# One copy for two heads' turned probabilities, and three steps moved in the order of the work

## The chip, the cores and the metric

The kernel runs on one core of one Trainium2 chip. The metric is the device time of one execution in microseconds (us); lower is better. A core has five engines that run side by side and wait for each other by semaphores: TensorE (PE in the rows, with its weight loads as PEld), VectorE (DVE), ScalarE (ACT), GpSimd (POOL) and SyncE (SP), which here only starts transfers. All of them share an on-chip memory of 128 partitions, the arena, and PE, DVE and ACT also reach PE's output memory, eight banks of 128 x 512 f32.

## The reference, cut to what matters

Two layers over 8 sequences of 512 tokens with 256 features. The first (a gated recurrence and a routed feed-forward net) is not touched. The second layer is, per sequence, a recurrence with a 16 x 16 state per head, times the SiLU of a block of attention and experts. Both read the normed input:

```python
x = x + s * g                        # s, g: the first layer's two branches
xn = _layernorm(x, axis=-1)
s = _L1_attn_ref(xn, ...)            # recurrence: state*w + k v, read out by r
g = _silu(_L1_ffn_ref(xn, ...))      # causal attention, then 8 experts + 1 shared
x = x + s * g
# inside _L1_ffn_ref, 16 heads, t = 512:
att = jnp.einsum('bhqd,bhkd->bhqk', q, k) / jnp.sqrt(jnp.float32(D))
att = jnp.where(mask, att, jnp.float32(-jnp.inf))
att = jax.nn.softmax(att, axis=-1)
y = jnp.einsum('bhqk,bhkd->bhqd', att, v)
```

## The kernel before, in words

Phases a and b compute the first layer and leave its branch `s` in rows in DRAM and its branch `g` sorted by expert in DRAM (`gate_rows`). Phase c computes the second layer, one sequence after another (`b` from 0 to 7). On each engine the order of the instructions is written out by hand and is strict; a wait holds up everything behind it on that engine. For each sequence phase c goes through three stages.

`before_attention` computes the projections. PE writes the last ones in the order of the list `QKV`: sp0, sp1, q2 to q7, lat. DVE turns each pair of heads' queries by their positions in `rotate` and so frees the bank. In between stand the first two attention steps: PE does `scores(b, 0)` after q5 and `scores(b, 1)` after q6, and DVE does the maxima of their rows, `highest(b, 0)` and `highest(b, 1)`, after its rotations of q5 and q6.

`attention` has 32 steps, `i` from 0 to 31. A step is one pair of heads (`i // 4`) and one tile of 128 queries (`qt = i % 4`), so that it has 1, 2, 3 or 4 tiles of 128 keys. Each step goes through these instructions:

- PE `scores(i)` (L1241, and the mask, L1244) into banks 0 and 1 or 2 and 3; it needs the exponentials of step i-2, which read the same banks.
- DVE `highest(i)` (L1822), one maximum for both heads.
- ACT `exp` (L1623), one instruction for each head, out of the bank into the arena, with the row sums.
- PE `turn_probs(i)` (L1258), `qt + 1` transposes for each head, head 0 into bank 5 and head 1 into bank 6.
- ACT `keep` (L1632), one copy for each head, out of the bank into the tile `turned`.
- PE `weigh_values` (L1295), in every second group of four steps, which multiplies the turned probabilities of four heads by the values.

PE's order in iteration i is `scores(i)`, `turn_probs(i - 2)`, `weigh_values(i - 3)` where there is one; ACT's is both copies of step i-2, then both exponentials of step i. Around this PE also reduces the recurrence's products (L1268), and DVE runs the 32 units of the recurrence, each a scan (L1842) and an outer product (L1835).

`experts` runs nine experts, `e` from 0 to 8. PE does `up(e)` and `down(e)` (L1382) and DVE `hidden(e)` (L1987, the product that `down(e)` needs), the sums of the experts' rows (L2073), and then `between(e)`: one or two units of the recurrence, and the head of the next sequence in pieces. `head_gate` (L1730) multiplies the rows of `s` by those of `g`, `head_sum` (L1734) adds the residual, `head_stats` (L1739) takes means and variances, `head_shift` (L1751) and `head_lerp` (L1764) come later. The rows of `g` are fetched by GpSimd with four indirect transfers (L2104), issued after its recurrence product of unit 24.

Of the kernel before, what the change touches and what calls it, by code (L numbers as in the profile page):

```python
# [11 lines left out]
ACT = mybir.ActivationFunctionType  # L12
X = mybir.AxisListType.X

P = 128
# [949 lines left out]
def phase_c(nc, io, dram, mem, const, psum, bank, pos_all, second, second_loads, weights_in, out):  # L965
# [3 lines left out]
    with ExitStack() as ctx:  # L969
# [42 lines left out]
        turned_at = mem.at  # L1012
        turned = [mem.take(NT, T) for _ in range(HGROUP)]
        neg_max, row_sum, row_inv = mem.take(STEPS), mem.take(STEPS), mem.take(STEPS)
# [140 lines left out]
        def _(pe):  # L1155
# [91 lines left out]
            def turn_probs(b, i):  # L1247

                qt = i % NT
                if i == 0:  # L1250
                    pe.wait_ge(v_read, pre.read(b, "q7"))
                for half in range(2):
                    s = 2 * i + half
                    pe.wait_ge(s_exp, STEPS * b + (s + 1))
                    if s >= 2:
                        pe.wait_ge(s_keep, STEPS * b + (s - 1))
                    for kt in range(qt + 1):
                        last = nc.tensor.transpose(bank[5 + half][:, kt * P:(kt + 1) * P], probs[s % PROBS][:, kt * P:(kt + 1) * P], ident)  # L1258
                    last.then_inc(s_turn, 1)
# [61 lines left out]
            def before_attention(b, ended):  # L1321
# [38 lines left out]
                for name in QKV:  # L1360
                    i = int(name[-1]) if name != "lat" else 0
                    if name[0] == "q":
                        query(b, i)
                        if name in ("q5", "q6"):
                            scores(b, int(name[1]) - 5)
                    elif name == "lat":
# [160 lines left out]
        def _(act):  # L1527
# [88 lines left out]
            def attention(b):  # L1616
# [8 lines left out]

                def keep(s):
                    i, half = s // 2, s % 2
                    h, qt = 2 * (i // NT) + half, i % NT
                    act.wait_ge(s_turn, STEPS * b + (s + 1))
                    if h >= HGROUP and h % HGROUP == 0:  # L1630
                        act.wait_ge(pv_mm, CHUNKS * b + (NT * (h // HGROUP - 1) + qt + 1) + CHUNKS)
                    nc.scalar.activation(turned[h % HGROUP][:, 0:qt + 1, qt * P:(qt + 1) * P],  # L1632
                                         bank[5 + half][:, 0:(qt + 1) * P].rearrange("p (k c) -> p k c", c=P),
                                         ACT.Copy).then_inc(s_keep, 1)

# [14 lines left out]
                for i in range(PSTEPS + LAG):  # L1650
# [6 lines left out]
                    if LAG <= i < PSTEPS + LAG:  # L1657
                        keep(2 * (i - LAG))
                        keep(2 * (i - LAG) + 1)
                    if i < PSTEPS:  # L1660
# [55 lines left out]
        def _(v):  # L1716
# [145 lines left out]
            def before_attention(b, ended):  # L1862
# [58 lines left out]
                for name in QKV:  # L1921
# [5 lines left out]
                    if name[0] == "q":  # L1927
                        rotate(m + 1)
                        if name in ("q5", "q6"):
                            highest(b, m - 5)  # L1930
                v.wait_ge(w_step, 2 * b + 2)
# [51 lines left out]
            def experts(b, final):  # L1983
# [46 lines left out]
                def between(e):  # L2030
                    if not final:
                        if e == 1:
                            head_gate(b + 1)
                        elif e == 2:
                            head_sum(b + 1)
                        elif e == 3:
                            head_stats(b + 1)
                    for n in EXPERT_UNITS.get(e, ()):
                        unit(b, n)
                    if not final:  # L2040
                        if e == 4:
                            head_shift(b + 1)
                        elif e == 6:
                            head_lerp(b + 1)
                    elif e == 6:
                        ln_inv(b, 0)
                    elif e == 7:
                        ln_scale(b, 0)
                        ln_gate(b, 0)
# [247 lines left out]
```

## Time and profile before

| | us |
|---|---|
| median of 3 runs | 2175.03 |
| lowest and highest run | 2170.23, 2177.49 |
| the profiled execution's own time | 2173.18 |
| its span, first to last instruction | 2171.3 |

The mean granted TensorE clock over the span is 0.971 of full speed. The span holds some 2 us less than the profiled execution's own time, and that execution lies 1.85 us below the median. Times in the rows are microseconds from the span's start.

### The profile page before, as it was taken

The numbers are of one execution on the slowest core, as the hardware profiler recorded it, in microseconds if no ns is written. First come the engines' busy times: TensorE is split into PE (matmuls) and PEld (weight loads), VectorE is DVE, ScalarE is ACT, GpSimd is POOL, SyncE is SP. The second block draws the span as 40 slices with busy tenths as digits, with TensorE's granted clock in tenths as the row PEclk, the third lists the DMA queues.
The fourth block names the chain that finished last, engine by engine and source line by source line (L and its number), as shares of the span: only waits on it lengthen the run. The fifth ranks groups of instructions, "written<-read, shape, count | busy, mean of one in ns | idle before, by whom it ended". The sixth has DMA issues, their size and how long they took to land.

```text
span 2171.3 us, 37412 instructions
## 1 busy us (share of the span) xinstructions
PE 2023.1 (93%) x11786; PEld 1237.3 (57%) x11787; DVE 1736.1 (80%) x2890; ACT 978.4 (45%) x2532; POOL 840.8 (39%) x666
## 2 busy tenths in 40 slices
PE   7998599999889999999999999999999999999996
PEld 4554399998446545644564465456445544654563
DVE  5998466665398888889978988888898788888886
ACT  3544244443247236623833472275238235723841
POOL 1335300000353345346334633553463346336531
PEclk9999799999799999999999999999999999999998
DMA  6544521211412212212321122123022211211220
GB/s 180 154 136 147 166 59 51 58 51 51 134 46 65 58 49 60 62 37 54 81 72 39 50 64 54 49 66 81 16 68 65 69 39 54 59 54 49 73 56 10
DMA packets 145728, 151.20 MB, mean 70 GB/s; under 512 B 47664, under 2 KB 105648, under 8 KB 145584
## 3 DMA queue, kind: packets, MB, share of 16 engines
q1 hardware_dynamic: 138288, 136.73, 22.8%
q0 software_dynamic: 3072, 8.41, 1.2%
q10 hardware_dynamic: 4224, 4.19, 0.7%
q8 instruction: 84, 1.38, 0.3%
q14 instruction: 60, 0.49, 0.1%
HBM read 121.71 MB, written 27.43 MB: 69 GB/s over the span
## 4 chain that ended last, share of the span: by engine, by line
PE 35%; issue 16%; POOL 10%; DVE 9%; ACT 3%; DMA 1%; POOLq 0%; DVEq 0%; ACTq 0%
PE bank L1382 8%; PE bank L1241 6%; PE bank L1258 5%; PE bank L1295 3%; PE bank L1395 3%; POOL arena L2131 3%; PE bank L1268 2%; POOL arena L2143 2%; POOL arena L2146 2%; DVE arena L1842 2%; PE bank L1244 2%; PE bank L1174 2%; ACT arena L1623 2%; POOL arena L2123 2%; DMA arena<-gate_rows,arena 1%
## 5 line engine op out<-in xcount | busy, mean ns | idle before, releaser
L2123 POOL TENSOR_TENSOR arena<-arena 128x512 f32<-128x512 f32 x256 | 341.1, 1337 | 559.1 <-DVE arena L1842 545.2
L1382 PE MATMUL bank<-arena 128*128 128x256 f32 (+1 forms) x1120 | 384.4, 498 | 20.5 <-DVE arena L1987 20.5
L1842 DVE TENSOR_TENSOR_SCAN arena<-arena 128x512 f32<-128x512 f32 x256 | 356.1, 1391 | 1.1
L1174 PE MATMUL bank<-arena 128*128 128x512 f32 (+2 forms) x768 | 350.8, 603 | 1.0 <-ACT arena L1562 1.0
L1623 ACT ACTIVATE arena<-bank,arena 128x128 f32<-128x128 f32 (+3 forms) x512 | 266.3, 530 | 171.1 <-DVE arena L1822 171.1
L1382 PEld LDWEIGHTS bank<-arena 128*128 128x128 f32 x1120 | 214.4, 195 | 179.0 <-issue 131.0
L1822 DVE TENSOR_REDUCE arena<-bank 128x2 f32<-128x256 f32 (+3 forms) x256 | 208.4, 814 | 51.7 <-PE bank L1244 51.0
L1241 PE MATMUL bank<-arena 64*128 64x128 f32 (+3 forms) x1024 | 208.2, 483 | 41.0 <-ACT arena L1623 28.2
L1174 PEld LDWEIGHTS bank<-arena 128*128 128x128 f32 (+2 forms) x768 | 138.0, 187 | 185.0 <-issue 164.4
L1835 DVE TENSOR_TENSOR arena<-arena 128x512 f32<-128x512 f32 x256 | 220.7, 864 | 11.7 <-DMA arena<-values 10.1
L1632 ACT ACTIVATE arena<-bank 128x128 f32<-128x128 f32 (+3 forms) x512 | 196.5, 439 | 40.2 <-PE bank L1258 39.3
L1258 PE MATMUL bank<-arena 128*128 128x128 f32 x1280 | 184.5, 275 | 2.3 <-DVE arena L1902 2.3
L283 PE MATMUL bank<-arena 128*128 128x512 f32 x384 | 174.3, 608 | 0.4 <-ACT arena L354 0.4
L1580 ACT ACTIVATE arena<-bank 128x512 f32<-128x512 f32 x72 | 42.7, 593 | 262.1 <-PE bank L1382 255.1
L1576 ACT ACTIVATE arena<-bank 128x512 f32<-128x512 f32 (+1 forms) x96 | 57.2, 596 | 213.9 <-PE bank L1174 213.7
L691 PE MATMUL bank<-arena 128*128 128x128 f32 x1248 | 147.8, 277 | 5.1 <-DVE arena L791 4.1
L691 PEld LDWEIGHTS bank<-arena 128*128 128x128 f32 x1248 | 147.3, 194 | 7.6 <-issue 4.4
L2146 POOL TENSOR_TENSOR arena<-arena 128x512 f32<-128x512 f32 x72 | 100.1, 1391 | 122.0 <-DVE arena L1905 118.8
L1241 PEld LDWEIGHTS bank<-arena 64*128 64x128 f32 x1024 | 77.8, 184 | 121.8 <-issue 49.6
L1258 PEld LDWEIGHTS bank<-arena 128*128 128x128 f32 x1280 | 137.7, 142 | 9.7 <-issue 6.1
L700 PE MATMUL bank<-arena 128*128 x624 | 141.1, 379 | 0.1
L354 ACT ACTIVATE arena<-bank 128x512 f32<-128x512 f32 x160 | 81.8, 611 | 109.2 <-PE bank L283 103.5
(207 smaller groups left out, 3032.4 us busy)
## 6 DMA issues: line engine op xcount, KB each, us to landing
arena<-values SPq DMA_DIRECT2D x256, 256.0 KB, 3.4
arena<-in_L_attn_h SPq DMA_DIRECT2D x16, 512.0 KB, 11.3
arena<-in_W1T SPq DMA_DIRECT2D x8, 1024.0 KB
arena<-in_W2T SPq DMA_DIRECT2D x8, 1024.0 KB
sorted_rows<-arena SPq DMA_DIRECT2D x42, 128.5 KB, 10.4
arena<-sorted_rows SPq DMA_DIRECT2D x40, 128.5 KB, 2.1
arena<-in_b2row SPq DMA_DIRECT2D x40, 128.0 KB, 2.9
gate_rows<-arena SPq DMA_DIRECT2D x39, 128.0 KB, 1.7
```

The costliest lines, as they stand in the source:

```text
L283: last = nc.tensor.matmul(bank[3 * (n % 2) + q][:, :], gru_w[layer][:, k, q * D + m * P:q * D + (m + 1) * P], source(b, u)[:, k, :], start ...
L691: last = nc.tensor.matmul(zT_bank[u % 2][half][:, (f % 4) * P:(f % 4 + 1) * P], w1_now[u % 2][:, c, f * P:(f + 1) * P], nT[u % 2][:, c, :] ...
L1174: last = nc.tensor.matmul(dst[rows, :], w, x, start=(n == 0), stop=(n == len(pairs) - 1))
L1241: nc.tensor.matmul(bank[2 * (i % LAG) + half][:, 0:n], qT[rows, p, qt * P:(qt + 1) * P], ckvT[rows, 0:n], start=True, stop=False)
L1258: last = nc.tensor.transpose(bank[5 + half][:, kt * P:(kt + 1) * P], probs[s % PROBS][:, kt * P:(kt + 1) * P], ident)
L1382: last = nc.tensor.matmul(dst[o], w, x, start=first, stop=last_one)
L1623: nc.scalar.activation(probs[s % PROBS][:, 0:n], bank[2 * (i % LAG) + half][:, 0:n], ACT.Exp, bias=neg_max[:, s:s + 1], accum_out=row_sum[ ...
L1632: nc.scalar.activation(turned[h % HGROUP][:, 0:qt + 1, qt * P:(qt + 1) * P], bank[5 + half][:, 0:(qt + 1) * P].rearrange("p (k c) -> p k c ...
L1822: nc.vector.tensor_reduce(neg_max[:, 2 * i:2 * i + 2], psum[:, at:at + 1024].rearrange("p (h k) -> p h k", h=2)[:, :, 0:n], X, ALU.max, ne ...
L1835: nc.vector.tensor_tensor(kv[n % 2], copies[n % COPIES], proj["k"][:, n // HD, :], ALU.mult).then_inc(kv_done, 1)
L1842: nc.vector.tensor_tensor_scan(state[n % STATES][:, 1:T + 1], proj["w"][:, m, :], kv[n % 2], VEC["init"][:, m * HD + j:m * HD + j + 1], AL ...
L2123: nc.gpsimd.tensor_tensor(prods[(n + 2) % PRODS], state[n % STATES][:, 0:T], proj["r"][:, m, :], ALU.mult).then_inc(prod_done, 1)
```

## The change

Four edits, without any arithmetic being added or left out:

- The two copies of a step become one: `keep(i)` reads banks 5 and 6 in one instruction and writes both heads' tiles. It waits for both heads' transposes, and raises its semaphore by 2. The four `turned` tiles become views of one tile at the same place.
- In `turn_probs` the wait for the copies of the step before stands once, ahead of the first head, and asks for both heads; before, each head waited for its own.
- `scores(b, 1)` moves from behind q6 to behind q7 on PE, and `highest(b, 1)` from behind the rotation of q6 to behind that of q7 on DVE.
- In `between`, `head_gate` moves from e = 1, ahead of unit 26, to e = 2, behind unit 27; `head_sum` moves from e = 2, ahead of unit 27, to e = 3, right ahead of `head_stats`, which stays.

```diff
-        turned = [mem.take(NT, T) for _ in range(HGROUP)]
+        turned_all = mem.take(HGROUP, NT, T)
+        turned = [turned_all[:, i, :, :] for i in range(HGROUP)]
...
                     pe.wait_ge(s_exp, STEPS * b + (s + 1))
-                    if s >= 2:
-                        pe.wait_ge(s_keep, STEPS * b + (s - 1))
+                    if i and half == 0:
+                        pe.wait_ge(s_keep, STEPS * b + 2 * i)
...
-                        if name in ("q5", "q6"):
-                            scores(b, int(name[1]) - 5)
+                        if name in ("q5", "q7"):
+                            scores(b, (int(name[1]) - 5) // 2)
...
-                def keep(s):
-                    i, half = s // 2, s % 2
-                    h, qt = 2 * (i // NT) + half, i % NT
-                    act.wait_ge(s_turn, STEPS * b + (s + 1))
+                def keep(i):
+                    h, qt = 2 * (i // NT), i % NT
+                    act.wait_ge(s_turn, STEPS * b + (2 * i + 2))
                     if h >= HGROUP and h % HGROUP == 0:
                         act.wait_ge(pv_mm, CHUNKS * b + (NT * (h // HGROUP - 1) + qt + 1) + CHUNKS)
-                    nc.scalar.activation(turned[h % HGROUP][:, 0:qt + 1, qt * P:(qt + 1) * P],
-                                         bank[5 + half][:, 0:(qt + 1) * P].rearrange("p (k c) -> p k c", c=P),
-                                         ACT.Copy).then_inc(s_keep, 1)
+                    at = h % HGROUP
+                    nc.scalar.activation(turned_all[:, at:at + 2, 0:qt + 1, qt * P:(qt + 1) * P],
+                                         psum[:, 5 * 512:7 * 512].rearrange("p (h k c) -> p h k c", h=2, c=P)[:, :, 0:qt + 1, :],
+                                         ACT.Copy).then_inc(s_keep, 2)
...
-                        keep(2 * (i - LAG))
-                        keep(2 * (i - LAG) + 1)
+                        keep(i - LAG)
...
-                        if name in ("q5", "q6"):
-                            highest(b, m - 5)
+                        if name in ("q5", "q7"):
+                            highest(b, (m - 5) // 2)
...
-                    if not final:
-                        if e == 1:
-                            head_gate(b + 1)
-                        elif e == 2:
-                            head_sum(b + 1)
-                        elif e == 3:
-                            head_stats(b + 1)
+                    if not final and e == 3:
+                        head_sum(b + 1)
+                        head_stats(b + 1)
                     for n in EXPERT_UNITS.get(e, ()):
                         unit(b, n)
+                    if not final and e == 2:
+                        head_gate(b + 1)
```

## Rows read from the trace of the kernel before

**Rows 1.** The page's busy times: engine, us (share of span), instructions.

```profile
PE 2023.1 (93%) x11786; PEld 1237.3 (57%) x11787; DVE 1736.1 (80%) x2890; ACT 978.4 (45%) x2532; POOL 840.8 (39%) x666
```

**Rows 2.** Who waited for whom, whole span: us in total, times, longest.

```profile
DVE arena L1730 <- DMA arena<-gate_rows,arena: 41.3, 8, 7.8
ACT arena L1632 <- PE bank L1258: 39.3, 60, 1.1
...
DVE arena L1788 <- PE bank L1306: 36.7, 8, 5.1
...
PE bank L1241 <- ACT arena L1623: 28.2, 57, 1.9
...
PE bank L1382 <- DVE arena L1987: 20.5, 8, 2.9
```

**Rows 3.** Timeline of DVE, experts of sequence 6: start, us, what [idle before, releaser].

```profile
1912.60 1.65 DVE L2073 SCALAR_TENSOR_TENSOR arena<-bank,arena 128x256 f32<-128x256 f32 x4
1919.07 1.23 DVE L1730 TENSOR_TENSOR arena<-arena 128x1024 f32<-128x1024 f32 x1 [4.83 <-DMA arena<-gate_rows,arena]
...
1929.24 1.40 DVE L1739 BATCH_NORM_STATS2 arena<-arena 128x6 f32<-128x256 f32 x4
...
1949.32 0.68 DVE L1987 TENSOR_TENSOR arena<-arena,bank 128x512 f32<-128x512 f32 x1
```

**Rows 4.** Timeline of PE in the same experts.

```profile
1909.22 10.60 PE L1382 MATMUL bank<-arena 128*128 128x256 f32 x32
1922.73 7.12 PE L1382 MATMUL bank<-arena 128*128 128x256 f32 x16 [2.90 <-DVE arena L1987]
...
1948.36 3.73 PE L1382 MATMUL bank<-arena 128*128 128x256 f32 x16
```

**Rows 5.** Stretches after the stall: us, PE, PEld, DVE, ACT, POOL busy, clock, DMA.

```profile
1131.95:1135.35 3.40, 3.34 (x8) 2.71 (x9) 3.40 (x7) 0.00 (x0) 0.35 (x1) 0.50 0.40 80
...
1330.21:1333.61 3.40, 3.35 (x12) 2.37 (x13) 3.40 (x6) 0.00 (x0) 0.35 (x1) 1.00 0.27 77
...
1922.67:1926.07 3.40, 3.34 (x9) 2.70 (x10) 3.40 (x7) 0.00 (x0) 0.36 (x1) 0.58 0.38 77
1926.07:1930.07 4.00, 4.00 (x13) 1.44 (x15) 4.00 (x10) 0.60 (x1) 1.46 (x1) 0.93 0.02 0
```

**Rows 6.** Timeline of PE, experts of sequence 3, after its stall.

```profile
1347.92 1.09 PE L1301 MATMUL bank<-arena 128*128 128x128 f32 x8 [0.63 <-ACT arena L1535]
1357.60 2.00 PE L1382 MATMUL bank<-arena 128*128 128x256 f32 x8 [0.48 <-DVE arena L1987]
```

**Rows 7.** The copies by shape, whole span: busy, mean ns, idle before.

```profile
L1632 ACT ACTIVATE arena<-bank 128x512 f32<-128x512 f32 x128 | 69.9, 597 | 21.4 <-PE bank L1258 21.4
...
L1632 ACT ACTIVATE arena<-bank 128x128 f32<-128x128 f32 x128 | 28.9, 285 | 17.8 <-PE bank L1258 17.8
```

**Rows 8.** Timeline of PE and ACT, attention steps 13 to 15 of sequence 6.

```profile
1837.75 1.04 PE L1258 MATMUL bank<-arena 128*128 128x128 f32 x8
...
1838.39 1.09 ACT L1632 ACTIVATE arena<-bank 128x512 f32<-128x512 f32 x2 [0.77 <-PE bank L1258]
...
1839.37 0.48 ACT L1623 ACTIVATE arena<-bank,arena 128x256 f32<-128x256 f32 x1
...
1840.44 1.13 PE L1241 MATMUL bank<-arena 64*128 64x512 f32 x4 [0.36 <-ACT arena L1623]
```

**Rows 9.** Timeline of PE and ACT, the last attention steps of sequence 6.

```profile
1877.45 0.84 PE L1258 MATMUL bank<-arena 128*128 128x128 f32 x6
...
1881.70 1.09 ACT L1632 ACTIVATE arena<-bank 128x512 f32<-128x512 f32 x2 [0.91 <-PE bank L1258]
```

**Rows 10.** Timeline of PE and DVE, the first attention steps of sequence 6.

```profile
1806.86 0.70 PE L1241 MATMUL bank<-arena 64*128 64x256 f32 x4 [1.03 <-DVE arena L1902]
...
1814.26 1.19 DVE L1822 TENSOR_REDUCE arena<-bank 128x2 f32<-128x1024 f32 x1
...
1816.99 0.87 PE L1241 MATMUL bank<-arena 64*128 64x256 f32 x4 [1.46 <-ACT arena L1623]
```

## The prediction, made before the changed kernel ran

> **What bounds the kernel now.** I read the busy times first [rows 1]. The reader should see that TensorE is busy for 93% of the span, and VectorE, at 80%, is the next. A cut elsewhere is worth only what TensorE stops waiting or stops running slowly. The list of waits says where TensorE waits [rows 2]: 28.2 us in 57 places for ScalarE's exponentials, and 20.5 us in 8 places for `hidden` on VectorE. Seven of those 8 follow a wait of VectorE itself, the 41.3 us in 8 places for the rows of `gate_rows` at `head_gate` (the eighth, of 7.8 us, stands ahead of the first sequence and is not touched).
>
> Then I read the timelines around both. In the experts of sequence 6 VectorE ends a sum at 1914.25 (1912.60 + 1.65), stands idle for 4.83 us until the gathered rows are there at 1919.07, and then works without a pause up to `hidden(8)` at 1949.32 [rows 3]. TensorE ends `up(4)` at 1919.82 (1909.22 + 10.60) and waits 2.90 us for `hidden(3)`, which stands behind the stall [rows 4]. The sixteen matmul records after the wait took 7.12 us; thirty-two before it took 10.60, or 5.3 for sixteen. The windows say why: the granted clock was 0.58 in the 3.4 us after the wait and 0.93 in the next 4 [rows 5], a mixture of 1.2 and 2.4 GHz. A stretch of length L at mean clock c costs (1 - c) x L against full speed, here 0.42 x 3.4 + 0.07 x 4 = 1.71 us. The same two windows after the other six stalls give 1.71, 1.71, 3.10, 0, 1.70 and 1.71; the clock of 0.50 and that of 1.00 are the extremes [rows 5]. Together 11.6 us.
>
> The stage after the experts begins with VectorE waiting for TensorE, 36.7 us in 8 places [rows 2]. So at the end of the experts TensorE is late, not VectorE, and time that TensorE saves there moves on into the next stage.
>
> **The gate and the sum moved.** No instruction is added or removed. Behind the sum that ends at 1914.25 VectorE now goes on with unit 26, `hidden(3)`, the next sums and unit 27. How long is that? From the gate at 1919.07 to `head_stats` at 1929.24 [rows 3] are 10.2 us: gate and sum at 1.2 us each, and twice one unit, one `hidden`, one group of sums. Half of the remaining 7.8 is 3.9, of which the sums are 1.6 and `hidden` 0.6 [rows 3], so a unit is 1.7. The gate stands at 1914.25 + 3.9 + 1.7 = 1919.9, and the rows were there at 1919.07. The transfers are issued by GpSimd behind unit 24, which the edit does not move. So the stall of 4.8 us should vanish, with 0.8 us to spare. Should the rows come somewhat later, the next that is late is `hidden(4)`, at about 1921.7, which TensorE needs only after `down(3)`, `up(5)` and a reduction, at about 1926: there are 4 us of cover.
>
> Is the whole stall then gain? TensorE runs from 1919.82 without the 2.90 and at full clock without the 1.71: its last matmul ends at 1947.5, not 1952.1. `down(8)` is the second half of the last 3.73 us [rows 4], so it starts at 1945.6. It needs `hidden(8)`, whose end moves by the stall from 1950.0 to 1945.2. That fits with 0.4 us to spare, so TensorE stays the bound, barely. Sequence 3 is the check: its clock never fell [rows 5], and it had 1.1 us of waits behind VectorE instead [rows 6], and its experts took as long as the others. Sum: seven waits of 2.86 us on average are 20.0, the clock 11.6, sequence 3's later waits 1.1, together 32.7 us less. The bounds are 7 x 3.6 = 25, if waits like those of sequence 3 come back everywhere, and 7 x 4.83 = 34, the whole stall.
>
> The Trainium skill (TensorE: Matmul & The Clock Gate, "HAM oscillation") says that idle gaps in TensorE's stream bring the low clock and that the restart pays for them. The trace agrees, six times of seven [rows 5]; without the clock's part the sum would be 21 us and not 33.
>
> **One copy for two.** 512 copies become 256. By shape a copy of 512 elements takes 597 ns and one of 128 takes 285 [rows 7]: 0.81 ns an element and 181 ns fixed. One instruction for 2 x 512 should take 181 + 832 = 1013 ns, against 1.09 us for the pair [rows 8], which already overlaps. So a step saves 0.07 us of ScalarE, 18 us over 256 steps, and for most of them ScalarE has idle time anyway (45% busy [rows 1]). The Trainium skill (ScalarE: Activation LUTs, "What ACT_TABLE_LOAD costs") gives a fixed cost of 186 ns and an overlap of 93 ns between neighbours. By its figures the saving would be 93 ns a step and 24 us in all, an estimate and again only of ScalarE's own time.
>
> The price is the start. A pair could begin when head 0 was turned; the one copy waits for head 1 too. At 1837.75 TensorE turns step 11 with eight transposes, the first copy starts at 1838.39 after a wait for the first four, and the exponential of step 13 starts at 1839.37 [rows 8]. The eighth transpose ends at 1838.79, so the one copy runs from 1838.83 to 1839.84, where the pair ended at 1839.48: the exponentials come 0.36 us later. `scores(15)` already waits 0.36 us for them [rows 8], so this is on the path. The pattern needs a step of four key tiles with no `weigh_values` behind it: steps 11, 19 and 27 (step 3 too, but there its successor has over 0.5 us of slack). Worked through the timelines, step 11's delay is partly taken back at the next wait for exponentials, leaving 0.2; step 19's stays, 0.36. At step 27 and the end, no scores come between the turns of steps 29 and 30, so TensorE waits for the copy itself at 1877.45 [rows 9], 0.65 in all. The last copy, at 1881.70 after 0.91 us of idle time [rows 9], ends 0.3 later and the last `weigh_values` waits 0.2. That is 1.4 us a sequence and 11.3 us over eight. Bounds: nothing, if small slack that I can't see takes it up, and 2.0 a sequence or 16 us, if each of the four places costs its full delay and a bit more. I take 11. The single wait of `turn_probs` for both copies asks nothing more, as the one copy ends both at once; merging the tiles into one moves no address.
>
> **The scores and the maximum moved.** TensorE's wait of 1.03 us ahead of `scores(1)` [rows 10] goes, since q7 fills it. But VectorE works without a pause through this stage, and the order of its instructions is all that changes there: `highest(3)` still starts at 1814.26, and the wait of 1.46 us ahead of `scores(5)` ends with the exponentials of step 3, which follow it [rows 10]. `highest(1)` comes 1.2 us later, and behind it on ScalarE stand the copies of step 0 and the exponentials of step 2. Those have about 0.9 us of idle time ahead of the exponentials of step 3 to catch up in. I take 0 us, with bounds of -0.3 and +0.3 a sequence, or 2.4 us each way.
>
> **Sum.** -32.7 + 11.3 + 0 = -21.4. The profiled execution's 2173.2 gives 2151.8. The median is 1.85 higher: 2153.6, rounded to 2153.
>
> **The rivals.**
> A, as above: 2153, with its own range 2146 to 2160.
> B, the one copy costs nothing, since the later exponentials are absorbed: 2175 - 33 = 2142. For it: in most of the 57 waits the exponential itself had waited for VectorE, not for a copy. Against it: the 0.36 of [rows 8] follows right behind the copy.
> C, VectorE becomes the bound of the experts: with 0.4 us to spare at `hidden(8)`, and sum and statistics now in one piece ahead of unit 28, waits of 1.1 us as in [rows 6] come in all seven: 2153 + 7.7 = 2161.
> D, the other sign: the one copy delays TensorE at every step by the second head's transposes, 0.11 us for each key tile, 1.1 us for a group of four steps, 8.8 a sequence, 70 in all: 2175 - 33 + 70 = 2212. It decides from 33 / 64 = 0.5 us a group on. For it: TensorE has hardly any slack. Against it: ScalarE stood idle for its transposes ahead of only 60 of 512 copies [rows 2]; elsewhere both heads had been turned long before.
> E, ScalarE's saved time lies on the path throughout: 2175 - 33 - 18 = 2124. Against it: the 57 waits are only 28.2 us in all, and the copies have no more than a share in them. The skill's saving of 93 ns would give 2118, by the rule above.
> F, the change does not do what it says: the gather is still late, or `head_sum` and `head_stats` in one piece hold up `hidden(5)` as long as the gate held up `hidden(3)`. Then only the copy's cost remains, 2175 + 0 to 11.
>
> **Chances.** A 0.50, B 0.17, C 0.17, D 0.06, E 0.05, F 0.05. Within 0.3% (6.5 us, about what a measurement of this kernel can tell from no change) falls half of F, 0.03. Slower are D and the rest of F, 0.08. Faster are A, B, C and E, 0.89. The range for 8 in 10 takes A, B and C with the bounds of the unknown costs: 2175 - 34 - 2 = 2139 below and 2175 - 25 + 16 = 2166 above; I take 2138 to 2166.
>
> **What would show it.** Right: no idle time ahead of L1730 in seven sequences, no wait of TensorE for L1987 in the middle of the experts, a clock of 1.00 there, and experts 4.6 us shorter. In attention, 256 copies of about 0.39 to 1.01 us, the wait ahead of `scores(15)` at about 0.7 us and not 0.36, and a stage longer by 1.4 us. Wrong: a new wait ahead of L1301 or of the last `down`, copies that take more than the sum of two, or an attention stage that is not longer. The most likely error is the size of the copy's price; the next is the clock, which follows idle time in ways that six cases of seven don't settle.

## The result and the profile after

The changed kernel takes 2181.34 us (median of 11 executions, lowest 2179.45), against 2174.68 us for the kernel before (11 executions beside it, 2167.43 to 2178.96). The ratio is 1.0034, 95% interval 1.0023 to 1.0045: slower by 7.4 us (the medians alone differ by 6.7), just past the 0.3% that can be told from no change. The forecast was 2153 us with a range of 2138 to 2166. One execution of 2630.08 us, and one of 5120.62 us in a later experiment, were disturbed and are left out of the ratios.

The profiled execution has a span of 2180.5 us (2171.3 before) at a mean clock of 0.969 (0.971), and its own time is 2182.27. The page's busy times, which answer to [rows 1]:

```profile
PE 2037.5 (93%) x11786; PEld 1242.7 (57%) x11787; DVE 1754.9 (80%) x2890; ACT 963.8 (44%) x2276; POOL 833.6 (38%) x666
```

ScalarE has 256 instructions and 14.6 us less. But VectorE, with the same 2890 instructions, is busy for 18.8 us more, and TensorE, with the same 11786, for 14.4 us more. Some instructions therefore take longer than they did. The list of waits of the changed kernel (us in total, times, longest), beside [rows 2]:

```profile
DVE arena L1788 <- PE bank L1307: 36.7, 8, 5.1
...
PE bank L1242 <- ACT arena L1624: 22.9, 42, 1.2
...
PE bank L1259 <- ACT arena L1633: 11.3, 45, 0.5
...
PE bank L1302 <- ACT arena L1536: 11.2, 8, 2.4
...
PE bank L1383 <- DVE arena L1987: 3.4, 7, 0.5
```

The 20.5 us of waiting for `hidden` are down to 3.4, and the wait of VectorE for `gate_rows` is gone in all seven places. TensorE waits 5.3 us less for the exponentials. In exchange it waits in 45 places for the copy itself ahead of `turn_probs` (L1259), where it had not waited at all, and 11.2 us ahead of L1302 (3.2 us in 2 places before), which turns the next sequence's normed input and comes after `head_stats` and `head_shift`.

**Stages.** Two instructions of VectorE mark two stages of a sequence. The attention stage runs from the start of L1788 to the start of L1936 (projections and attention), the experts' stage from there to the next L1788. The first L1936 has no L1788 ahead of it, so seven attention stages have a length; the low clock is counted for all eight. In the table the attention stage is given for sequences whose clock stayed at 1.00 in it, and where there are several, as the shortest of them. Low clock is counted as in the prediction, (1 - c) x L summed over windows of 4 us in the 92 us ahead of L1936.

| | before | after |
|---|---|---|
| attention stage at clock 1.00, us | 119.48 (five, to 119.82) | 121.38 (one) |
| sequences of 8 with low clock there, and how much | 3, 1.7 us each | 6 with 3.4 us, 1 with 1.7 |
| attention stage in these, us | 120.74 | 123.0 to 123.4; 122.06 |
| experts' stage, us | 77.12 to 77.22, once 78.50 | 75.21 to 75.24 |
| last experts' stage, us | 69.60 | 70.04 |

Over the seven experts' stages with a successor the changed kernel is 14.9 us shorter. Over the seven attention stages behind them it is 19.7 us longer, the last experts are 0.4 longer, and the first L1936 starts 3.7 us later. That is +8.9 of the 9.2 us between the spans. The 3.7 are not all the change's: in the profiles of all fourteen kernels of this document the first L1936 starts between 694.8 and 701.0 us (697.3 before, 701.0 here).

**Where half of the gate's gain went.** VectorE's timeline in the experts of sequence 6, beside [rows 3] (everything in this sequence stands 7.2 us later than in the kernel before):

```profile
1924.16 1.65 DVE L2071 SCALAR_TENSOR_TENSOR arena<-bank,arena 128x256 f32<-128x256 f32 x4
1925.73 2.76 DVE L1842 TENSOR_TENSOR_SCAN arena<-arena 128x512 f32<-128x512 f32 x1
1928.41 0.66 DVE L1835 TENSOR_TENSOR arena<-arena 128x512 f32<-128x512 f32 x1
1929.00 2.11 DVE L1730 TENSOR_TENSOR arena<-arena 128x1024 f32<-128x1024 f32 x1
...
1936.38 1.28 DVE L1842 TENSOR_TENSOR_SCAN arena<-arena 128x512 f32<-128x512 f32 x1
```

GpSimd's timeline in the same stretch:

```profile
1924.11 0.94 POOL L2102 DMA_INDIRECT arena<-gate_rows,arena  x1 [0.30 <-issue]
1925.07 2.33 POOL L2121 TENSOR_TENSOR arena<-arena 128x512 f32<-128x512 f32 x2
1928.57 1.46 POOL L2121 TENSOR_TENSOR arena<-arena 128x512 f32<-128x512 f32 x1 [1.17 <-DVE arena L1842]
```

The second of the two products in the row of 1925.07, taken by itself:

```profile
1926.30 1.10 POOL L2121 TENSOR_TENSOR arena<-arena 128x512 f32<-128x512 f32 x1
```

And TensorE's, beside [rows 4, 6]:

```profile
1945.60 1.09 PE L1302 MATMUL bank<-arena 128*128 128x128 f32 x8 [1.26 <-ACT arena L1536]
...
1955.27 2.00 PE L1383 MATMUL bank<-arena 128*128 128x256 f32 x8 [0.49 <-DVE arena L1987]
```

VectorE has no idle time ahead of `head_gate`, as forecast. But the scan of unit 27 takes 2.76 us, where an undisturbed one takes 1.28 (the last row of VectorE's), and the gate takes 2.11 us, where it took 1.23 [rows 3]. Both run beside GpSimd: its products of units 25 and 26 had piled up behind the four transfers and run back to back from 1925.07 to 1927.40, and the next runs from 1928.57 to 1930.03. The scan overlaps the first pair for 1.67 us and is stretched by 1.48; the gate overlaps the next product for 1.03 us and is stretched by 0.88. This makes 2.36 us of the 4.8 that the stall took. In the kernel before, the product of unit 25 ran from 1917.15 to 1918.42, while VectorE stood idle for the gathered rows, and those of units 26 and 27 one at a time, at 1921.65 and 1926.65, and neither the gate nor the scans of units 26 and 27 were stretched. TensorE now waits 1.26 + 0.49 us in these experts.

The Trainium skill (SBUF — State Buffer, "Who interferes with whom") says that a VectorE instruction with two inputs in the arena contends with a GpSimd instruction that reads it, for a port pair that only one of them holds at a time, and that the order in which they are issued decides who is blocked. The lengths in the trace agree to within 0.2 us: blocked until 1927.40 and then 1.28 long, the scan would end at 1928.68, and ended at 1928.49; the gate would end at 1931.26, and ended at 1931.11. Read with the starts in the trace, the order does not agree. The product of unit 26 started at 1926.30, 0.57 us after the scan, and yet ran its 1.10 us while the scan was held. The next product started during L1835 and got in ahead of the gate; an experiment below has the same starts to within 0.01 us and the other outcome in six of seven sequences.

**Where the copy costs.** By shape, the copies of the changed kernel, beside [rows 7]:

```profile
L1633 ACT ACTIVATE arena<-bank 128x1024 f32<-128x1024 f32 x64 | 66.0, 1031 | 59.9 <-PE bank L1259 36.2 <-issue 23.7
...
L1633 ACT ACTIVATE arena<-bank 128x256 f32<-128x256 f32 x64 | 24.8, 387 | 5.0 <-PE bank L1259 2.8
```

The same place as in [rows 8], ScalarE of sequence 6 first and then TensorE:

```profile
1844.11 1.03 ACT L1633 ACTIVATE arena<-bank 128x1024 f32<-128x1024 f32 x1 [1.11 <-issue]
1845.04 0.46 ACT L1624 ACTIVATE arena<-bank,arena 128x256 f32<-128x256 f32 x1
```

```profile
1842.99 1.04 PE L1259 MATMUL bank<-arena 128*128 128x128 f32 x8
...
1845.29 0.41 PE L1259 MATMUL bank<-arena 128*128 128x128 f32 x2 [0.20 <-ACT arena L1633]
...
1846.10 1.13 PE L1242 MATMUL bank<-arena 64*128 64x512 f32 x4 [0.40 <-ACT arena L1624]
...
1884.62 0.85 PE L1259 MATMUL bank<-arena 128*128 128x128 f32 x6 [0.48 <-ACT arena L1633]
```

From the start of the turn of step 11 to `scores(15)` it is now 1846.10 - 1842.99 = 3.11 us, where it was 1840.44 - 1837.75 = 2.69 [rows 8]. That is 0.42 us, where 0.36 was worked out. The delay shows in two waits, 0.20 ahead of the next turn and 0.40 ahead of the scores, not in the one of 0.7 that was forecast. The last row is the turn of step 30, which follows its predecessor without `scores` between them.

**The clock.** Windows of 2 us in the first attention steps of sequence 5 (columns as in [rows 5]), and TensorE's timeline there, beside [rows 10]:

```profile
1616.00:1618.00 2.00, 1.92 (x14) 1.16 (x13) 1.97 (x2) 0.06 (x1) 1.47 (x2) 1.00 0.02 4
1618.00:1620.00 2.00, 0.60 (x2) 0.29 (x2) 2.00 (x6) 0.05 (x1) 1.83 (x2) 0.65 0.00 0
1620.00:1622.00 2.00, 1.07 (x3) 0.51 (x4) 1.97 (x2) 2.00 (x9) 1.92 (x2) 0.50 0.00 0
1622.00:1624.00 2.00, 2.00 (x10) 0.85 (x6) 0.53 (x1) 0.53 (x2) 2.00 (x2) 0.50 0.03 8
1624.00:1626.00 2.00, 2.00 (x14) 1.42 (x12) 2.00 (x4) 1.62 (x4) 2.00 (x3) 0.64 0.04 0
```

```profile
1614.93 0.70 PE L1242 MATMUL bank<-arena 64*128 64x256 f32 x4
...
1619.40 0.69 PE L1259 MATMUL bank<-arena 128*128 128x128 f32 x2 [1.48 <-DVE arena L1902]
1621.02 2.08 PE L1242 MATMUL bank<-arena 64*128 64x512 f32 x4 [0.93 <-ACT arena L1624]
...
1626.37 0.70 PE L1242 MATMUL bank<-arena 64*128 64x256 f32 x4 [0.25 <-ACT arena L1624]
```

The wait ahead of `scores(1)` is gone, as meant, and the 1.46 us ahead of `scores(5)` [rows 10] are down to 0.25. In their place TensorE waits 1.48 us ahead of the first turn and 0.93 ahead of `scores(3)`, with 0.7 us of work between them. The clock falls to 0.50, that is 1.2 GHz, at about 1618.6, during the first of them, and is back at 1.00, 2.4 GHz, some 7 us later. The four matmul records of `scores(3)` (two matmuls, with two records each) take 2.08 us, where the same four at full clock take 1.13 (the row of `scores(15)` above). In the other sequences such a pair of waits (0.86 to 1.51 us, then 0.93 to 1.19) stands there too, but the clock falls at different points: before the second wait, in it or, in sequence 6, 1.2 us behind it, and in sequence 1, with waits of 0.89 and 1.18, not at all.

### The profile page after: what moved, and what is told of

Read it like the earlier page. It is cut to its first block, busy times and chain, and to the rows that moved or that the text cites. A ratio compares the mean times of both kernels' runs of the same rounds, so it can differ in the third digit from the quotient of the medians.

```text
span 2180.5 us, 37068 instructions
## 1 busy us (share of the span) xinstructions
PE 2037.5 (93%) x11786; PEld 1242.7 (57%) x11787; DVE 1754.9 (80%) x2890; ACT 963.8 (44%) x2276; POOL 833.6 (38%) x666
## 4 chain that ended last, share of the span: by engine, by line
PE 45%; issue 11%; DVE 9%; ACT 4%; POOL 4%; DMA 0%; ACTq 0%; POOLq 0%; DVEq 0%
PE bank L1383 14%; PE bank L1242 6%; PE bank L1175 5%; PE bank L1259 5%; ACT arena L1624 3%; PE bank L1296 3%; PE bank L1396 3%; PE bank L1269 3%; PE bank L1245 2%; PE bank L1453 1%; POOL arena L2129 1%; PE bank L1281 1%; DVE arena L1866 1%; ACT arena L1633 1%; DVE arena L1822 1%
## 5 line engine op out<-in xcount | busy, mean ns | idle before, releaser
L2121 POOL TENSOR_TENSOR arena<-arena 128x512 f32<-128x512 f32 x256 | 330.6, 1297 | 571.3 <-DVE arena L1842 556.6
L1383 PE MATMUL bank<-arena 128*128 128x256 f32 (+1 forms) x1120 | 374.1, 486 | 3.4 <-DVE arena L1987 3.4
L1842 DVE TENSOR_TENSOR_SCAN arena<-arena 128x512 f32<-128x512 f32 x256 | 363.8, 1421 | 1.1
L1242 PE MATMUL bank<-arena 64*128 64x128 f32 (+3 forms) x1024 | 215.8, 499 | 26.2 <-ACT arena L1624 22.9
L1835 DVE TENSOR_TENSOR arena<-arena 128x512 f32<-128x512 f32 x256 | 222.2, 870 | 11.6 <-DMA arena<-values 10.0
L1633 ACT ACTIVATE arena<-bank 128x256 f32<-128x256 f32 (+3 forms) x256 | 181.2, 708 | 98.5 <-PE bank L1259 63.3
L1259 PE MATMUL bank<-arena 128*128 128x128 f32 x1280 | 192.8, 283 | 20.0 <-ACT arena L1633 11.3
L1259 PEld LDWEIGHTS bank<-arena 128*128 128x128 f32 x1280 | 141.7, 145 | 33.8 <-issue 23.2
L691 PE MATMUL bank<-arena 128*128 128x128 f32 x1248 | 148.5, 277 | 5.1 <-DVE arena L791 4.1
L2144 POOL TENSOR_TENSOR arena<-arena 128x512 f32<-128x512 f32 x72 | 102.5, 1423 | 121.9 <-DVE arena L1905 118.7
```

The costliest lines, as they stand in the source:

```text
L691: last = nc.tensor.matmul(zT_bank[u % 2][half][:, (f % 4) * P:(f % 4 + 1) * P], w1_now[u % 2][:, c, f * P:(f + 1) * P], nT[u % 2][:, c, :] ...
L1242: nc.tensor.matmul(bank[2 * (i % LAG) + half][:, 0:n], qT[rows, p, qt * P:(qt + 1) * P], ckvT[rows, 0:n], start=True, stop=False)
L1383: last = nc.tensor.matmul(dst[o], w, x, start=first, stop=last_one)
L1633: nc.scalar.activation(turned_all[:, at:at + 2, 0:qt + 1, qt * P:(qt + 1) * P], psum[:, 5 * 512:7 * 512].rearrange("p (h k c) -> p h k c", ...
L1835: nc.vector.tensor_tensor(kv[n % 2], copies[n % COPIES], proj["k"][:, n // HD, :], ALU.mult).then_inc(kv_done, 1)
L1842: nc.vector.tensor_tensor_scan(state[n % STATES][:, 1:T + 1], proj["w"][:, m, :], kv[n % 2], VEC["init"][:, m * HD + j:m * HD + j + 1], AL ...
```

## The experiments

Each ratio is against the kernel before, with its 95% interval, and a difference to it in us is the ratio's; the medians of the kernel before beside them were 2174.15 (the first four), 2172.41 (the next four) and 2174.35 us (the last four). Experts' stages and attention stages are those defined above, each read from one profiled execution of the kernel; where the attention stages at clock 1.00 differ, the shortest is given.

**The parts alone.** Only the hunk in `between`:

```diff
+                    if not final and e == 3:
+                        head_sum(b + 1)
+                        head_stats(b + 1)
                     for n in EXPERT_UNITS.get(e, ()):
                         unit(b, n)
+                    if not final and e == 2:
+                        head_gate(b + 1)
```

> Before, with head_gate and head_sum moved alone. Theory 1 (each edit has its own price; VectorE became the bound of the experts because the scan of unit 27 and the gate now run beside GpSimd's products): experts of 75.2 us in place of 77.2, seven times, so 14 us less than before in all, 2161; the gate takes 2.1 us and TensorE waits some 1.3 us for the norm of the next sequence. Theory 2 (the gain is only held back by the one copy): the full 4.6 us a sequence, 33 us less, 2142.

Measured: 2152.68 us, 0.9905 [0.989, 0.9919], so 20.7 us faster, between the 14 of the one theory and the 33 of the other. The gate takes 2.11 us in all seven sequences and the experts' stages are 74.8 us, 2.4 shorter than before. They sum to 17.9 us; 2.2 more come from the attention stages, of which one of eight has low clock and not three.

Only the merged copy, with `turned_all`, the one wait and `keep(i)`:

> Before, with the one copy and its single wait on TensorE alone. Theory 1: the later start costs 2.0 us a sequence in attention and 0.4 behind it, 19 us in all, 2194, and the granted clock at the start of attention stays as before. Theory 2 (the copy costs what was predicted, 1.4 us a sequence, and the rest is TensorE's clock at the start of attention): 2186.

Measured: 2191.65 us, 1.008 [1.0066, 1.0094], 17.4 us slower. The attention stage at clock 1.00 is 121.47 us (the longest of six 122.45), 2.0 longer than before, and the experts' stage 77.6, 0.44 longer. The low clock comes ahead of two of eight L1936, against three before.

Only `scores(b, 1)` and `highest(b, 1)` moved behind q7:

> Before, with scores(b, 1) and highest(b, 1) behind q7 alone. Theory 1: the two waits of TensorE that take the place of one bring the low clock at the start of attention in most sequences and for longer, and the stage gets 0.5 to 1.5 us longer: 4 to 12 us more, about 2182. Theory 2 (the low clock needs the one copy as well): no difference to before, 2175.

Measured: 2176.43 us, 1.0012 [1.0002, 1.0023], 2.6 us slower. The low clock comes as the first theory says, but at less than its price: all eight attention stages have 3.4 us of it, and the seven that can be measured last 120.7 to 121.2 us. The experts' stages are 77.1 to 77.2 us although in six of seven the clock was 1.00 throughout them. In the kernel before most of them had 1.7 us of low clock and the same length.

The gate, the sum and the scores, without the merged copy:

> The changed kernel with two copies as before: scores, maximum, gate and sum moved. Theory 1 (prices add up): 14 less and 7 more, about 2168. Theory 2: 2142 plus nothing.

Measured: 2156.04 us, 0.9919 [0.9905, 0.9932]. Put beside the first of these kernels, the moved scores bring nothing; the median is 3.4 us higher, with intervals that overlap. All eight attention stages have low clock, seven of them 1.7 us, and last 119.7 to 120.1 us, so that this much of it costs some 0.25 us a stage here.

**What in the copy costs.** The kernel before, its two copies kept, but each waiting for both heads, and one wait in `turn_probs`:

```diff
-                    if s >= 2:
-                        pe.wait_ge(s_keep, STEPS * b + (s - 1))
+                    if i and half == 0:
+                        pe.wait_ge(s_keep, STEPS * b + 2 * i)
...
-                    act.wait_ge(s_turn, STEPS * b + (s + 1))
+                    act.wait_ge(s_turn, STEPS * b + (2 * i + 2))
```

> Before, still with two copies a step, but each waits for the transposes of both heads, and TensorE's single wait stands ahead of the first head. Theory 1 (the one copy is slow because it starts later): the pair starts as late and takes 1.09 us where the one copy takes 1.03, so at least as slow as the one copy alone, 2192 to 2196. Rival (the instruction itself is what costs: two banks in one access): close to before, 2175.

Measured: 2192.89 us, 1.0096 [1.0074, 1.0117]. So having to wait, for ScalarE's copies and in TensorE's `turn_probs`, costs by itself what the merged copy costs, and the instruction saved is worth at most 0.2 us a sequence (an attention stage of 121.66 us against 121.47).

The merged copy in all steps but those of four key tiles, which keep their two:

```diff
-                        keep(2 * (i - LAG))
-                        keep(2 * (i - LAG) + 1)
+                        if (i - LAG) % NT == NT - 1:
+                            keep(2 * (i - LAG))
+                            keep(2 * (i - LAG) + 1)
+                        else:
+                            keep_both(i - LAG)
```

> Before, with the one copy in the steps of one to three key tiles and two copies in those of four. Theory 1 (the later start costs where eight transposes stand ahead of the copy and the exponentials behind it): most of the 17 us of the one copy is gone, 2175 to 2180. Rival (the price is paid at every step): three quarters of it stay, 2188.

Measured: 2178.93 us, 1.0029 [1.0015, 1.0042]. The attention stage is 120.3 us, 0.85 longer than before, and the experts' stage is as before (but for the last, 70.08 us). So the steps of four tiles carry 1.15 of the 2.0 us and all of the 0.44, and the smaller steps, which were forecast to cost nothing but their share at the end, carry 0.85: 0.35 by `scores(31)` and 0.50 ahead of the turn of step 30.

**Gate, sum and merged copy, the scores back in their old place:**

> The changed kernel with scores(b, 1) and highest(b, 1) back behind q6. Theory 1 (the scores' move brings the low clock at the start of attention in nearly every sequence, and costs more in company than its 2 us alone): the gate's 21 less and the copy's 17 more, about 2171, with little low clock at the start of attention. Rival (the prices of gate and copy do not add up by themselves): about 2181, as the changed kernel.

Measured: 2176.91 us, 1.002 [1.0007, 1.0032]. The changed kernel stands at 1.0034, so the moved scores cost it some 3 us, with intervals that overlap. The time lies between the two theories: the gate's 20.7 less and the copy's 17.4 more would be 3.3 us faster than before, and this is 4.3 slower. In the profiled execution two of eight attention stages have low clock, 1.7 us each; the others last 121.45 to 121.83. That execution took 2173.84 us, 3 less than the median. Over the twelve executions the time goes with the mean clock of the whole span: 2172.9 to 2174.8 us in the four at 0.978, 2176.6 to 2181.0 in the five at 0.974 or 0.975.

**The cause of the stall instead of its place.** The kernel before, with nothing changed but GpSimd's order: the four indirect transfers are issued ahead of product 23 and not behind product 24.

```diff
-                for n in range(EARLY + 1, EXPERT_UNITS[0][-1]):
-                    product(b, n)
                 if not final:
                     g.wait_ge(pv_mm, CHUNKS * b + 2 * CHUNKS)
                     gather(b + 1)
+                for n in range(EARLY + 1, EXPERT_UNITS[0][-1]):
+                    product(b, n)
```

> Before, with GpSimd's four indirect transfers issued ahead of its product of unit 23 in place of behind that of unit 24; gate and sum where they were. Theory 1 (the stall of 4.8 us ends with the gather, and moving the gate gave back only 2.4 us of it since scan and gate then ran beside GpSimd's products 25 and 26): the stall goes and the scan of unit 27 and the gate stay at 1.3 and 1.2 us; TensorE becomes the bound, experts of some 73.3 us against 77.2, 27 us less in all, 2148. Rival (the experts have another bound at 74.8): 2153, as with the gate moved.

Measured: 2136.53 us, 0.9838 [0.9817, 0.986], 35 us faster, more than the 27 expected. VectorE's timeline in the experts of sequence 6:

```profile
1882.28 1.21 DVE L1730 TENSOR_TENSOR arena<-arena 128x1024 f32<-128x1024 f32 x1
1883.41 1.27 DVE L1842 TENSOR_TENSOR_SCAN arena<-arena 128x512 f32<-128x512 f32 x1
```

The gate stands where it always stood, with no idle time, and neither it nor the scan behind it is stretched. The experts' stage is 72.43 us, 4.7 shorter than before, except for one of 74.13, in which the gate waited 1.60 us for another transfer, that of the rows of `s`.

**The low clock of the changed kernel.** The changed kernel with nine filler matmuls of 128 x 128 (18 records), four behind `scores(2)` and five ahead of `scores(3)`, which write into a bank that is not in use there and change no output:

```diff
+                def fill(n):
+                    pe.wait_ge(last_read, 4 * b + 1)
+                    for _ in range(n):
+                        nc.tensor.matmul(whole[:, 0:P], ident, ident, start=True, stop=True)
```

> The changed kernel with nine extra 128 x 128 matmuls a sequence (0.1 us each), whose result nobody reads, in the two waits of TensorE at the start of attention: four ahead of the transposes of step 0 and five ahead of the scores of step 3. Theory 1 (the scores' move costs through the low clock that its two waits bring): the clock stays at 1.00 there, the stage goes from 123.1 to 121.4 us in the sequences that had it, 10 us less than the changed kernel, 2171. Rival (the stage is longer by waits, the clock only goes with them): no gain or a loss, 2181 or more.

Measured: 2170.19 us, 0.9984 [0.9975, 0.9993]. Its TensorE in sequence 5:

```profile
1609.38 1.11 PE L1405 MATMUL bank<-arena 128*128 128x128 f32 x8
1610.45 0.44 PE L1259 MATMUL bank<-arena 128*128 128x128 f32 x2
1610.73 1.28 PE L1405 MATMUL bank<-arena 128*128 128x128 f32 x10
1612.07 1.13 PE L1242 MATMUL bank<-arena 64*128 64x512 f32 x4
```

The fillers (L1405) stand where the waits were. Four take 1.11 us and five 1.28, so 0.26 to 0.28 each and not the 0.1 of the expectation. No attention stage has low clock, and the stages last 121.34 to 121.72 us. With work of no use added, the kernel is 11 us faster than the changed one (2181.34 - 2170.19).

**The changed kernel with the early transfers of the experiment above:**

> The changed kernel with the gather issued ahead of GpSimd's product of unit 23. Theory 1 (what the moved gate lacked came from scan and gate running beside GpSimd's products 25 and 26, which the late gather had pushed together): the scan of unit 27 takes 1.28 us and not 2.76, the gate 1.2 and not 2.1, and the experts go from 75.2 to some 72.8 us, 17 us less than the changed kernel, 2164. Rival (sum and statistics in one piece hold the experts at 75): 2181.

Measured: 2165.78 us, 0.9964 [0.9951, 0.9977]. VectorE and, below, GpSimd in the experts of sequence 6:

```profile
1911.36 1.27 DVE L1842 TENSOR_TENSOR_SCAN arena<-arena 128x512 f32<-128x512 f32 x1
1912.56 0.67 DVE L1835 TENSOR_TENSOR arena<-arena 128x512 f32<-128x512 f32 x1
1913.14 1.22 DVE L1730 TENSOR_TENSOR arena<-arena 128x1024 f32<-128x1024 f32 x1
```

```profile
1908.85 1.37 POOL L2121 TENSOR_TENSOR arena<-arena 128x512 f32<-128x512 f32 x1 [2.39 <-DVE arena L1842]
1912.71 2.59 POOL L2121 TENSOR_TENSOR arena<-arena 128x512 f32<-128x512 f32 x1 [2.49 <-DVE arena L1842]
```

Scan and gate are short again, in the same order on VectorE as in the changed kernel, and the experts' stage is 73.01 us and not 75.24. GpSimd's products no longer pile up, so they end before the scan begins. The one that starts during L1835 and meets the gate is itself the one that is stretched, to 2.59 us; TensorE's timeline shows no wait in these experts. One of the seven gates, that of 1520.94, took 2.11 us, and that stage 73.9. GpSimd's product there:

```profile
1520.51 1.46 POOL L2121 TENSOR_TENSOR arena<-arena 128x512 f32<-128x512 f32 x1 [2.49 <-DVE arena L1842]
```

It started 0.43 us ahead of the gate, as the product of 1912.71 did and as that of 1928.57 did in the changed kernel. With starts as alike as these, either the product or the gate was held; what decides which is not shown.

In attention nothing is repaired: all eight stages have low clock, 1.7 or 3.4 us. This kernel is 29 us slower than the kernel before with the same early transfers (2165.78 - 2136.53). Once the rows come in time, the four edits together only cost.

**Further on from the early transfers.** With the load of the rows of `s` also issued earlier (unit 26 instead of 28 in SyncE's order), and with that and nine fillers ahead of `scores(5)`:

> The kernel before with the early gather of the last call, and the loads of the next sequence's rows at unit 26 of SyncE's loop in place of unit 28. It had one wait of 1.60 us of VectorE for those rows, which made the experts of one sequence 1.7 us longer. Theory 1: that wait goes, all experts take 72.4 us, 2135 to 2136. Rival: more transfers at once delay the values of the recurrence, 2138 or more.

> As e11, with nine extra 128 x 128 matmuls a sequence whose result nobody reads in TensorE's wait ahead of the scores of step 5. Theory 1 (the low clock follows that wait in some sequences and costs 1.3 us each time): no low clock in attention, 2 to 4 us less, 2132. Rival (the matmuls outlast the wait): 2 to 4 us more.

Measured: 2138.77 us, 0.9839 [0.9823, 0.9855], and 2138.21 us, 0.9839 [0.9825, 0.9854]. Both do in the profile what they were made for: all seven experts' stages last 72.4 us in both, and with the fillers only the first sequence has low clock. Neither came to the expected time (2135 to 2136, and 2132): it is that of the early transfers alone. The fillers cost 0.2 us a sequence (119.65 against 119.47), which takes up what the clock gives back in the few sequences that had lost it.

## Why the prediction was wrong, step by step

| term | predicted, us | alone, us | 
|---|---|---|
| gate and sum | -32.7 | -20.7 |
| one copy | +11.3 | +17.4 |
| scores and maximum | 0 | +2.6 |
| sum of the three | -21.4 | -0.7 |
| all together, measured | | +7.4 |

The forecast is off by 28.8 us (-21.4 against +7.4): 12.0 of it are the gate's, 6.1 the copy's, 2.6 the scores', and 8.1 what the parts bring together and not alone.

**The stall: right.** The rows are there when the moved gate needs them. The gate's forecast start, 1919.9, is 38.6 us behind L1936 of that sequence; it started 40.57 behind it. The difference is 1.48 of the stretched scan and 0.44 that the copy brings into this stage.

**"So it starts at 1945.6. That fits with 0.4 us to spare, so TensorE stays the bound": this step failed.** It took every instruction of VectorE at the duration it had before. Two of them became 1.48 and 0.88 us longer, because they now ran where VectorE had stood idle, beside GpSimd's products. VectorE became the bound of the experts, with waits of TensorE of 1.26 and 0.49 us. VectorE as the bound is rival C, but C gave another reason for it and put it at 1.1 us a sequence, where it was 2.4. The early transfers show it from both sides: with scan and gate undisturbed the changed kernel's experts' stage falls from 75.24 to 73.01 us. The view that would have told it is GpSimd's timeline, which was not read: what runs there while VectorE stands idle, since that is the time into which work is moved.

**The size of the whole stall: right, its split wrong.** The waits and the clock together were put at 32.7 us, or 4.7 a sequence. The kernel before with early transfers, in which nothing is stretched, gains 4.7 us in the experts' stage, nearly the whole stall. That the sum came out is in part luck, since the clock was not a gain beside the waits. The kernel before has experts' stages of 77.12 us both where the clock never fell (sequence 3) and where it cost 1.7 us (sequence 5), and with only the scores moved they are as long although the clock is 1.00 in six of seven. At full clock TensorE comes earlier to what VectorE makes, and waits for it, as in [rows 6]. Nor is (1 - c) x L a price elsewhere: 1.7 us of low clock lengthened an attention stage by 1.26 us in the kernel before and by some 0.25 in the kernel with scores, gate and sum moved. What counts is how much earlier VectorE gets there: 4.7 us without the stretching, 2.4 with it.

**One copy: right mechanism, wrong size.** The copy of 1024 elements takes 1.031 us (1.013 forecast) and starts when it was forecast, and having to wait is the whole price, as the pairs that wait show. Predicted were 1.4 us a sequence. The stages show 2.0 + 0.44 (the start behind L1936 included). In the profile of the kernel with the copy alone, beside that of the kernel before, `scores` of steps 15, 23 and 31 come 0.43, 0.43 and 0.42 later and the turn of step 30 half a microsecond; smaller steps add 0.5 by step 31 and 0.3 is taken back. So the four places of the forecast came to 0.43 (0.2 forecast), 0.43 (0.36), 0.42 + 0.49 (0.65) and 0.44 (0.2), and 0.2 more came from the rest. "The pattern needs a step of four key tiles" failed by that last part, since steps of fewer tiles also passed their delay on; the larger part is that each place was sized too small. "The single wait of `turn_probs` asks nothing more" is doubtful too, since TensorE now waits there 45 times. How much of that is the wait and how much the later copy was not told apart, because the pairs that wait had both.

**The scores: 0 was right for the work, wrong for the clock.** At clock 1.00 the attention stage is 121.38 us with the scores moved and 121.47 without. The wait ahead of `scores(5)`, forecast to stay at 1.46 us, is 0.67 in the one sequence at full clock. But two waits now lie close together ahead of `scores(3)`, and the low clock comes in seven of eight sequences, in six of them for twice as long; in the two other kernels with only the scores, or the scores and the gate, moved it comes in all eight. The Trainium skill (TensorE: Matmul & The Clock Gate, "A second HAM failure mode: psum-queue depth-cycling") tells of short idle gaps between groups of matmuls that bring the low clock. The trace agrees in part: waits of 0.86 to 1.51 us went with the low clock in seven sequences, and filling them took it away, but in sequence 1 waits of 0.89 and 1.18 passed at full clock.

**Why the parts don't add up.** Alone they come to -0.7 us, together to +7.4. By stages and at clock 1.00 they do add up: an attention stage of 119.48 + 2.0 - 0.1 = 121.4, measured 121.38; an experts' stage of 74.8 + 0.44 = 75.24, as measured. With the fillers, where no attention stage has low clock, the changed kernel is 3.5 us faster than the kernel before (0.9984), which is about the sum of gate and copy, -3.3. So the rest goes with the low clock, 11 us in the changed kernel. It is not the moved scores alone that bring it: gate and copy without the scores are 4.3 us slower than before, 7.6 above their sum, and their executions are the longer the lower their clock. In the profiled executions the gate's move alone had low clock in one attention stage of eight, the copy alone in two, gate and copy together in two, the kernel before in three, and the changed kernel in seven, and for longer. Why gate and copy together lose more than each alone was not found: their profiled execution is one of the short ones. What decides, for waits as alike as these, whether the clock falls and for how long stays open too.

## What to carry to other kernels

When an engine waits for a transfer, look first at what holds up the transfer's issue. Issuing it earlier gave 35 us here, and moving the waiting instruction 21; with both, and the rest of the change, it was 8. Before work is moved into an engine's idle time, read the timelines of its neighbours for that time: with two inputs in the arena on VectorE and products on GpSimd the moved work may not run at its old duration. Merging two instructions on an engine with time to spare gained nothing here and made the first half wait for the second's data, at 17 us. Judge each stage with its clock apart: whether two waits of TensorE were filled or not decided over 11 us in the whole.

## What the runs showed of the hardware

- A scan of 128 x 512 with two inputs in the arena took 1.28 us alone and 2.76 beside two GpSimd products, of which one had begun 0.66 us before it and the other 0.57 us after it. A product of 128 x 1024 took 1.23 and 2.11. Where a GpSimd product started 0.43 us ahead of that product and during the VectorE instruction before it, one of the two was held: VectorE's, at 2.11 us with GpSimd's at 1.46, in all seven sequences of the changed kernel and one of the kernel with early transfers; GpSimd's, at 2.59 with VectorE's at 1.22, in the other six.
- TensorE's waits of 1.48 and 0.93 us with 0.7 us of work between them went with 1.2 GHz for some 7 us, from 0.7 us into the first wait on. Nine matmuls of 128 x 128, 0.26 to 0.28 us each, in such places kept 2.4 GHz in all eight sequences; waits of 0.89 and 1.18 us passed at 2.4 GHz in one sequence.
- One ScalarE copy across two banks takes what a copy of as many elements within one takes: 600 and 387 ns for 512 and 256 elements, against 597 and 383; for 1024 and 768 elements it takes 1031 and 813 ns.
